# A new order of the attention step on four engines, projections in halves, memory read-out ahead of the value products

## The reference, cut to what matters

```python
scores = where(mask, -inf, q @ k.T / 8)              # per sequence and head, 128 x 128
att_dot = softmax(scores) @ v
sq, sk = elu(q) + 1, elu(k) + 1
att_mem = (sq @ M) / (sq @ Z.T)                      # M: 64 x 64 memory, Z: 1 x 64
M, Z = M + sk.T @ v, Z + sk.sum()                    # for the next segment
att = gate * att_mem + (1 - gate) * att_dot
out = att.reshape(B, 128, 1024) @ Wo
```

## Time and profile before

| | us |
|---|---|
| median of 3 runs | 1071.33 (1067.80 to 1072.13) |
| profiled execution | 1069.13 |
| its span, first to last instruction | 1067.3 |
| TensorE busy | 989.8 (93%) |
| VectorE busy | 780.9 (73%) |
| ScalarE busy | 634.6 (59%) |
| GpSimd busy | 577.8 (54%) |
| mean granted TensorE clock | 0.98 of full |

### The profile page before, as it was taken

The page is one execution under the profiler, slowest core; times in us unless marked ns, Lnnn a source line. Parts: engine busy times, 40 slices in busy tenths (PEclk is TensorE's granted clock), DMA queues, the critical chain, the costliest instruction groups (busy, mean ns, idle before and its releaser), DMA issues.

```text
span 1067.3 us, 20188 instructions
## 1 busy us (share of the span) xinstructions
PE 989.8 (93%) x7748; PEld 697.6 (65%) x7748; DVE 780.9 (73%) x1400; ACT 634.6 (59%) x1364; POOL 577.8 (54%) x688
## 2 busy tenths in 40 slices
PE   5999999999999999999999999999999889999971
PEld 2677777776777777767777777777777765343431
DVE  6868686867787877777777777686868463588685
ACT  4756565556566564556565646574746354687872
POOL 4456565446565654456565634565656352455573
PEclk9999999999999999999999999999999899999995
DMA  7100000000000000000000000000000100300025
GB/s 187 32 21 1 21 2 20 3 22 1 21 2 21 2 20 2 21 2 21 1 21 2 21 2 20 2 21 1 12 2 10 24 11 10 157 1 1 1 44 115
DMA packets 17038, 23.92 MB, mean 22 GB/s; under 512 B 7472, under 2 KB 9264, under 8 KB 16432
## 3 DMA queue, kind: packets, MB, share of 16 engines
q1 hardware_dynamic: 15472, 18.58, 6.3%
q10 hardware_dynamic: 1472, 4.06, 1.1%
HBM read 13.97 MB, written 8.65 MB: 21 GB/s over the span
## 4 chain that ended last, share of the span: by engine, by line
PE 72%; DVE 18%; POOL 3%; ACT 3%; issue 3%; POOLq 0%; DVEq 0%; ACTq 0%
PE ps L1241 18%; PE ps L1347 11%; PE ps L1305 6%; PE ps L1282 5%; PE ps L1488 4%; PE ps L1475 4%; DVE arena L915 4%; PE ps L1311 3%; PE ps L1292 3%; PE ps L1332 3%; PE ps L1470 3%; PE ps L1257 3%; DVE arena L875 2%; PE ps L1319 2%; DVE arena L940 2%
## 5 line engine op out<-in xcount | busy, mean ns | idle before, releaser
L1241 PE MATMUL ps<-arena 128*128 128x512 f16 x1152 | 266.7, 382 | 5.1 <-DVE arena L892 3.0
L660 ACT ACTIVATE arena<-ps,arena 128x128 f32<-128x128 f32 x512 | 139.4, 387 | 96.1 <-DVE arena L940 96.1
L1241 PEld LDWEIGHTS ps<-arena 128*128 128x128 f16 x1152 | 110.3, 98 | 126.1 <-DVE arena L915 4.5
L915 DVE STREAM_TRANSPOSE arena<-ps 128x1024 f32<-128x1024 f32 x96 | 145.6, 1517 | 24.6 <-PE ps L1241 22.5
L468 POOL TENSOR_TENSOR arena<-arena 128x256 f32<-128x256 f32 x128 | 93.2, 729 | 123.2 <-DVE arena L950 82.0
L1305 PE MATMUL ps<-arena 128*128 128x65 f32 x1024 | 135.9, 276 | 5.9 <-ACT arena L667 4.8
L1305 PEld LDWEIGHTS ps<-arena 128*128 128x128 f32 x1024 | 127.4, 192 | 18.8 <-ACT arena L667 8.3
L867 DVE BATCH_NORM_STATS2 arena<-arena 128x6 f32<-128x256 f32 x100 | 36.9, 410 | 121.0 <-ACT arena L686 120.2
L1347 PE MATMUL ps<-arena 128*128 128x256 f32 x544 | 121.9, 382 | 0.0
L453 POOL TENSOR_TENSOR arena<-arena 128x512 f32<-128x512 f32 x48 | 73.2, 1525 | 86.6 <-ACT arena L653 86.6
L1347 PEld LDWEIGHTS ps<-arena 128*128 128x128 f32 x544 | 102.0, 190 | 15.7 <-ACT arena L674 0.8
(11 more groups left out here) (120 smaller groups left out, 1788.3 us busy)
## 6 DMA issues: line engine op xcount, KB each, us to landing
x_rows<-arena SPq DMA_DIRECT2D x17, 256.0 KB, 2.0
arena<-x_rows SPq DMA_DIRECT2D x4, 1024.0 KB, 7.8
arena<-in_L_attn_x_dram SPq DMA_DIRECT2D x124, 32.0 KB, 1.8
out_dram<-arena SPq DMA_DIRECT2D x18, 128.0 KB, 3.1
arena<-in_L_attn_Wq_dram ACTq DMA_DIRECT2D x2, 512.0 KB, 4.3
arena<-in_L_attn_Wk_dram ACTq DMA_DIRECT2D x2, 512.0 KB, 6.8
arena<-in_L_attn_Wv_dram ACTq DMA_DIRECT2D x2, 512.0 KB, 8.3
arena<-in_L_attn_Wo_dram SPq DMA_DIRECT2D x8, 128.0 KB, 4.6
```

The costliest lines, as they stand in the source:

```text
L660: last = act.activation(Pr[:, par, j, :], s_bank[:, par, j * P:(j + 1) * P], ACT.Exp, bias=negm[:, par, j:j + 1])
L915: dve.transpose(dst[:, d0:d0 + 32], bank.rearrange("p w (d c) -> p d w c", c=C)).then_inc(x_free, 1)
L1241: last = pe.matmul(bank[:, w, :], xc[:, lx, k, w * P:(w + 1) * P], W16[lw][:, k, i, :], start=(n == 0), stop=(n == 5))
```

## The change

It reorders the calls of `step` on TensorE, VectorE, ScalarE and GpSimd. To do so it cuts some helpers in parts:

- ScalarE's `take_q` becomes `exp_q` (Q) and `high_k` (K); `probs` and `take_p` handle one parity per call; `take_p` counts `p_copied` once per parity, in place of `p_done` once per group.
- VectorE's `maxima` handles one parity per call, `to_rows` one half.
- TensorE's `read_out` becomes `recall` (memory read-out), `values` and `remember` (memory products), in this order; `project` can do one row half. All matmuls stay as they were.
- `STEP_JOBS` has Q2 ahead of Y, so Q2 takes the bank of Q1, A0, A2 and K2, and Y that of A1, A3 and N.
- `attT` lies on `nat` instead of in memory of its own.

```diff
-STEP_JOBS = ["Q1", "K1", "A0", "A1", "A2", "A3", "Y", "Q2", "K2", "N", "Q3", "K3", "F", "Q0", "K0"]
+STEP_JOBS = ["Q1", "K1", "A0", "A1", "A2", "A3", "Q2", "Y", "K2", "N", "Q3", "K3", "F", "Q0", "K0"]
-        attT = alloc(2 * H * DK).rearrange("p (w j r) -> p w j r", w=2, j=8)
+        attT = nat.rearrange("p w e c -> p (w e c)").rearrange("p (w j r) -> p w j r", w=2, j=8)
 # GpSimd, step
-                    elu_k(bp, s, 0)
                     if m > 0:
                         gated(*before(bp, s), 3, 0)
                         gated(*before(bp, s), 3, 1)
+                    elu_k(bp, s, 0)
                     elu_k(bp, s, 1)
                     gated(bp, s, 0, 0)
-                    gated(bp, s, 0, 1)
                     if m < NT - 2:
                         deviation(n_rs, n_mv, n_stat, n_rstd, m + 3)
+                    elu_k(bp, s, 2)
                     y_dev(bp, s)
+                    gated(bp, s, 0, 1)
+                    residual(bp, s)
+                    x2_dev(bp, s)
+                    elu_k(bp, s, 3)
                     gated(bp, s, 1, 0)
...
 # ScalarE
+                def take_p(bp, s, g, par):
+                    act.wait_ge(pt_full, bp * 32 + 8 * s + 2 * g + par + 1)
+                    act.activation(PT[:, par].rearrange("p j i -> p (j i)"), s_bank[:, par, :],
+                                   ACT.Copy).then_inc(p_copied, 1)
...
 # TensorE
+                def recall(bp, s, g, half):
+                    pe.wait_ge(pm_free, bp * 32 + 8 * s + 2 * g + half + 1)
+                    if s == 0:
+                        pe.wait_ge(m_reset, bp * 8 + 2 * (g + 1))
...
+                def values(bp, s, g, half):
+                    pe.wait_ge(p_copied, 2 * (G + 1))
...
+                    if half == 0 or s == NSEG - 1:
+                        last.then_inc(pm_full, 1)
+                def remember(bp, s, g):
+                    if s == NSEG - 1:
+                        return
+                    pe.wait_ge(sk_done, sk_count(bp, s, g) + 2)
...
+                    last.then_inc(pm_full, 1)
```

More of the change, by code:

```diff
@@ L1047, in step @@
                     divide(bp, s, 2, 0)
-                    maxima(bp, s, 3)
-                    seq_sums(bp, s)
-                    divide(bp, s, 2, 1)
+                    maxima(bp, s, 3, 0)
+                    maxima(bp, s, 3, 1)
                     if not last:
                         take_x(bp, s, 4)
+                    divide(bp, s, 2, 1)
+                    seq_sums(bp, s)
+                    if not last:
                         take_q(bp, s, 0)
@@ L1236, in project @@
                     xc = xcur[par]
-                    for w in range(2):
+                    for w in ws:
                         n = 0
@@ new lines, in values @@
+                def values(bp, s, g, half):
+                    G = bp * 16 + 4 * s + g
+                    v = v_pos[s % 2].rearrange("p (y r h e) -> p y h r e", y=2, r=2, h=HP)[:, g // 2]
+                    pe.wait_ge(p_copied, 2 * (G + 1))
+                    for u in range(4):
+                        j, par = 2 * half + u // 2, u % 2
+                        last = pe.matmul(pm_bank[:, 0, u * DV1:(u + 1) * DV1], PT[:, par, j, :],
+                                         v[:, GP * (g % 2) + j, par, 0:DV1], start=True, stop=True)
+                    if half == 0 or s == NSEG - 1:
+                        last.then_inc(pm_full, 1)
@@ new lines, in remember @@
+                def remember(bp, s, g):
+                    if s == NSEG - 1:
+                        return
+                    v = v_pos[s % 2].rearrange("p (y r h e) -> p y h r e", y=2, r=2, h=HP)[:, g // 2]
+                    pe.wait_ge(sk_done, sk_count(bp, s, g) + 2)
+                    for a in range(GP):
+                        h = GP * (g % 2) + a
+                        for par in range(2):
+                            unit = 2 * (GP * (g - g % 2) + h) + par
+                            last = pe.matmul(pm_bank[64 * par:64 * par + 64, a // 2,
+                                                     (4 + a % 2) * DV1:(5 + a % 2) * DV1],
+                                             sk[:, DK * unit:DK * (unit + 1)], v[:, h, par, 0:DV1],
+                                             start=True, stop=True)
```

220 lines of the change are left out of this document (113 added, 107 removed).

## The result

The changed kernel takes 1037.37 us (median of 4 runs, 1034.96 to 1039.36) against 1069.78 for the kernel before in the same comparison: 0.9695 of its time, 95% interval 0.9659 to 0.9731. The forecast was 1045, range 1034 to 1062. The profiled execution is one of the longer ones, 1039.14 us (span 1037.4), 30.0 less than the profiled one before.

The account below looks back on a forecast made before the run. TensorE sets the pace, losing 33 us over fifteen steps; 33 - 6.8 still lost + 4.7 from the last step = 31, giving 1038; 4.5 for thin crossings and 2.5 for the clock make 1045 us, range 1034 to 1062.

Parts of the forecast that it names:

- The walk: New order followed through the engines' queues from a step's first scores: 0.45 us lost per step, 31 us gained, 1038.
- crossings that hold by 0.2 or less: Six places per step where data arrives at most 0.2 us before it is due; charged 0.3 per step, 4.5 us.
- The hop behind exponentials: In the head, from ScalarE's exponentials to TensorE's transposes of the probabilities: taken as 0.17 us.
- small waits at projection 5's first half and at K0: In a step's tail on TensorE, expected as signs of the new order; K0's wait for the sequence sums was 0.12 us.
- Cuts: Splitting three projections per step by row halves on TensorE: taken as 0 per cut, from above 4.5 us in all.
- F behind scores 3: In the tail, FFN rows' transposes placed after scores 3, due at 42.9 us, so their 0.97 us wait goes.
- The last step: Last attention step, without projections to cover its head: ends 4.7 us earlier, 2.5 of that lost if the clock drops.
- Rival 1: Head chain of seven hops and the tail run 0.1 us longer per hop: 15 us given back, 1060; chance 0.18.
- Rival 3: Late group 0 exponentials make TensorE wait at the probabilities and again at the A transposes: slower, 1077; chance 0.08.
- rival 2: No change, 1069: small losses spread over the step until they refill the 1.87 us won; chance 0.08.
- rival 4: The whole gain comes and the clock holds: 1038 or less, down to 1033; chance 0.04.
- three signs of being wrong: Head's transposes later than 7.5 us after the scores, a half projection starting with its own gap, step above 52.5.

Follow-up runs that it names:

- the first experiment: The changed kernel with projections 2, 4 and 5 whole again, each at the place of its first half: 1071.33 us, ratio 1.0009 to the kernel before.
- the fourth experiment: The changed kernel with the FFN rows' transposes ahead of scores 3 again: 1042.03 us, ratio 0.9732 to the kernel before.
- the two delays: The changed kernel with four, then fifteen, small scratch copies on ScalarE ahead of group 0's exponentials: 1042.57 us and 1058.93 us.
- the filled kernel of before: The kernel before with 9 extra matmuls, results unused, ahead of scores 1 in its last attention step: 1068.74 us against 1071.44.

## Why the prediction was right, and which steps were not

**What bounds the kernel, and the ceiling.** Right, and close. Starts, not busy bars, gave 33 us to win in fifteen steps; 30.0 were won, and 33.5 by the kernel with the exponentials first. So the 33 was no strict ceiling: "51.3 us of an ordinary step stay" was 0.2 too high, as 51.11 shows. TensorE's own work did not change: weight-load busy time in the ordinary step is 39.91 after 39.41. The Trainium skill (Perfetto Trace Analysis, Identifying the Most-Contended Engine) points to weight-load busy time as a measure of headroom. By it 11.4 us of "room" (51.34 minus 39.91) would still be there, though the trace has no gap to take them from.

**The walk.** It gave 1038, and I set 1045 by charging 4.5 us for crossings that hold by 0.2 or less, and 2.5 for the clock. That 1038 is so near is partly luck: the fifteen steps gained 30.0 where the walk had 26.2 (it left 0.45 us per step, and 0.2 stayed), and the last step lost 0.9 where it had 4.7 to gain. The thin crossings held in the ordinary steps: 51.34, below the walk's 51.4 to 51.5 and below the 51.5 to 51.9 that I named as the sign, so the charge of 4.5 us was for nothing. The hop behind exponentials, which I took as 0.17 without a row of its own, was too long: the first turned probabilities start at 6.78 where I had 6.92, at the undisturbed 0.44 behind K1 (295.21 to 295.65). The wait does not show there, but some 0.2 us show in the next three blocks (295.65 to 297.18 is 1.53, where the kernel with the exponentials first has 1.32), so the 0.24 that the walk lost at the head was about right. The forecast of small waits at projection 5's first half and at K0 failed for s=1 and 2. At s=3 the first of them is there, 0.60 idle for VectorE's take 4 (L929), since no memory products stand ahead; this is the row of the changed kernel at m = 11:

```profile
639.80 1.47 PE L1260 MATMUL ps<-arena 128*128 128x512 f16 x6 [0.60 <-DVE arena L929]
```

**Cuts.** Cost at nothing: right. But the prediction stopped there. What the halves bring (without them all of the gain is gone, by the first experiment) stood in it only as "now hides", with no price.

**F behind scores 3, "the 0.97 is gone".** The wait is gone, the reason was wrong. In the fourth experiment F stands ahead of scores 3 again and doesn't wait. What took the wait away is the distance between VectorE and TensorE: low Q3 is ready at 40.6 us, and in the new order TensorE reaches this place at 41.6. The move itself is worth 4.7 us (1042.03 minus 1037.37) by another way: scores 3 start earlier, and with them the maxima, take 4 and projection 5.

**s=0, banks, GpSimd.** The 1.37 wait for low K1 is gone, and the s=0 step gained 3.1, all that the prediction had found lost in it. Q2 ahead of Y is worth 11.5 us. The order of GpSimd's head and the shared buffer are worth nothing measurable.

**The last step.** Walked as 4.7 shorter, with 2.5 set against it for the clock. The walk was right where the clock stayed up: the same step takes 45.88 us in the kernel with GpSimd's old head and 45.85 in the one with whole projections (whose edit does not touch the last step), and against 50.36 before that is 4.5. Of these 4.5 some 1.3 are the clock's: the kernel before fell to half for 6.8 us, and with filler and full clock its last step took 49.10. The order alone brings about 3.2. In the profiled execution after the change the clock was at half for 10.2 and 3.5 us, and all of it was gone. The term that was mis-sized is the clock's: 5.35 us (51.23 minus 45.88) instead of 2.5. Over the runs of the changed kernel the times follow the clock: 1039.1 and 1039.4 at a mean of 0.978, 1035.0 and 1035.6 at 0.983 and 0.981.

**Rivals.** Rival 1 rests on seven hops without slack: the chain has none, as the two delays show, but the hops were not longer than taken (6.78 against 6.92 at its end). Rival 3's second wait does not come up to 1.5 us of delay. In the two experiments that end at the time of before (whole projections, values first) the loss spreads over four waits in a step, as rival 2 described it for the changed kernel. The median, 1037.37, lies inside the range of rival 4 (1033 to 1038) as well as in that of the forecast, but rival 4 wanted the clock held, and in at least half of the runs it was not. None of the three signs of being wrong came: 6.78 instead of over 7.5, no gap before a half, 51.34 instead of over 52.5.

The 30 us are not a sum of parts. Undoing the halves costs 34, undoing the read-out's place 36, the bank order 11.5, F's place 4.7: 86 together by medians, and 34.7, 30.0, 11.5 and 5.7 by the fifteen steps. Undoing either of the first two takes the whole gain away, so neither has a share of its own. That this is so because the order has almost no slack is my reading; no run tests it apart from the head chain.

## What to carry to other kernels

Where one engine sets the pace, add up its pitches from start to start and compare with the step: the difference is about what an order can win (33 us here, 30.0 and 33.5 were won). A walk through the four queues, made with durations and hops from the rows, then gave the ordinary step within 0.2 us. Cut long blocks and keep small ones that need little (here the read-out) to stand where the next product is still being copied; then look at which jobs share a bank and so wait for each other, since a bank order alone was worth 11 us. The last step of a loop, which has no work for a next step to fill its waits, must be looked at apart: its waits can cost twice, once by themselves and once by the clock behind them.

## What the runs showed of the hardware that was not expected

The granted clock falls in some executions and not in others, for the same kernel: the one with GpSimd's old head took 1033.2 us at a mean clock of 0.983 and 1039.1 at 0.978. After the same 2.4 us idle stretch in the last step the changed kernel's profiled run went to half clock (1.2 GHz) for 10.2 us, the kernel with GpSimd's old head stayed at full (2.4 GHz). In every profiled execution the falls inside the sixteen steps lie in or shortly behind an idle stretch of TensorE, the shortest of these 1.0 us. In the changed kernel these are two waits of the last step, with falls at 804.3 and 828.2 us:

```profile
804.12 0.93 PE L1313 MATMUL ps<-arena 128*128 128x128 f32 x4 [2.42 <-ACT arena L662]
827.21 1.11 PE L1333 MATMUL ps<-arena 128*128 128x65 f32 x8 [1.81 <-ACT arena L668]
```

In the filled kernel of before the clock fell once in the middle, at 257.2 us, in an s=0 step right behind the wait for low K1. TensorE was busy during the fall. First the wait, then busy time by stretch of that execution, the s=0 step (53.67 us otherwise) and the 3.4 us in it:

```profile
256.56 0.40 PE L1270 MATMUL ps<-arena 64*64 64x512 bf16 x2 [1.37 <-DVE arena L925]
```

```profile
244.20:299.48 55.28, 52.76 (x449) 40.38 (x448) 40.42 (x75) 33.51 (x74) 32.92 (x40) 0.97 0.04 11
257.20:260.60 3.40, 3.40 (x33) 3.20 (x27) 2.43 (x4) 1.15 (x3) 3.23 (x4) 0.50 0.02 5
```

The profiled execution of the kernel before has the same wait at the same place (1.38 us, 256.70) and no fall behind it. What sets off such a fall stays open: the falls come with idle stretches, and filling them lowered the time in both kernels, but an idle stretch doesn't decide it alone.
